# Transposes of the first half of the attention weights emitted before two quantisation slots and half of P·V, in an AdaLN transformer layer on eight cores

## The reference

```python
mod = (_silu(c) @ wmod).reshape(4, 6, 1, -1)          # sa, ca, ga, sb, cb, gb
h = _layernorm(x) * (1 + ca) + sa
k = h @ Wk.T ; q = h @ Wq.T ; v = h @ Wv.T
ak = k @ Wa.T
alpha = softmax(q @ ak.T)                             # 4096 x 4096 in each sequence
out = alpha @ (v @ Wb.T)
x = x + ga * out
h = _layernorm(x) * (1 + cb) + sb
# per-tensor: wq = clip(round(w / scale), -128, 127) * scale, scale = max|w| / 127
h = gelu(h @ quant(W_fc).T + b_fc + 2 * (h @ A_fc.T) @ B_fc.T)
x = x + gb * (h @ quant(W_proj).T + b_proj + 2 * (h @ A_proj.T) @ B_proj.T)
```

## Time and profile before

| | us |
|---|---|
| median of the timed runs (2) | 3236.74 |
| lowest, highest | 3222.4, 3251.07 |
| the profiled execution, device time | 3184.89 |
| its span on the slowest core (core 5) | 3183.3 |
| the spans of its eight cores | 3171.0 to 3183.3 |
| attention stage within that span, from the first eA to the last PV1 | 1233.4 to 2317.5 |

### The profile page before, as it was taken

How to read it: one execution, slowest core, us unless ns; L and a number is a source line. 1 busy time by engine, 2 the same in 40 slices (tenths; PEclk the granted TensorE clock), 3 DMA queues, 4 the chain that set the end, 5 groups by cost and what they waited for, 6 DMA issues and landing times.

```text
span 3183.3 us, 24979 instructions; the slowest of 8 cores (3171.0 to 3183.3 us)
## 1 busy us (share of the span) xinstructions
PE 1730.6 (54%) x7994; PEld 764.1 (24%) x7994; DVE 1001.1 (31%) x1773; ACT 763.1 (24%) x1325; POOL 432.7 (14%) x585
## 2 busy tenths in 40 slices
PE   3620040426666556455664465654526858858588
PEld 1210010112222222222222222222212323323233
DVE  3420333434444543444344434344311020110201
ACT  2310001032222231333233333233303122031220
POOL 0001222213333100111111112112200000000000
PEclk9855575757787768777777777777757979979799
DMA  4500424232222220121112212112151113112130
GB/s 142 169 13 5 139 86 136 71 116 69 68 70 68 70 63 30 53 73 70 60 57 77 72 60 73 57 58 78 60 167 54 59 51 95 60 50 63 47 99 27
DMA packets 92297, 233.40 MB, mean 73 GB/s; under 512 B 25380, under 2 KB 25509, under 8 KB 92152
## 3 DMA queue, kind: packets, MB, share of 16 engines
q1 hardware_dynamic: 65000, 160.33, 16.8%
q0 software_dynamic: 27168, 71.47, 6.4%
HBM read 193.85 MB, written 37.88 MB: 73 GB/s over the span
## 4 chain that ended last, share of the span: by engine, by line
PE 33%; DMA 23%; DVE 15%; issue 12%; ACT 10%; POOL 4%; SPq 1%; DVEq 1%; ACTq 0%; POOLq 0%
PE pO L1436 7%; DMA amst<-wpj_in 6%; PE pO L1198 5%; PE pE L1394 5%; PE pE L1101 5%; DMA wfcst<-wfcq_sc 4%; PE pE L1126 4%; ACT h_stage L729 3%; DVE qkf L960 2%; DMA wm<-wmod_in 2%; POOL qt L936 2%; DMA amst<-wfc_in 2%; PE pE L742 2%; ACT qkf L930 2%; DMA bfcT_sc<-lora 2%
## 5 line engine op out<-in xcount | busy, mean ns | idle before, releaser
L936 POOL TENSOR_TENSOR qt<-qt,qkf 128x1024 f32<-128x1024 f32 x64 | 149.9, 2342 | 939.5 <-ACT qkf L930 911.3
L1394 PE MATMUL pE<-h,wfcst 128*128 128x512 bf16 x1024 | 248.6, 386 | 51.8 <-DMA wfcst<-wfcq_sc 39.1
L1436 PE MATMUL pO<-wpj_sb,hid 128*128 128x512 bf16 x1024 | 226.4, 379 | 15.8 <-DVE outb L1452 12.0
L1101 PE MATMUL pE<-ak_fm,q_stg 128*128 128x512 bf16 x512 | 148.9, 462 | 142.2 <-DMA q_stg<-q_sc 110.0
L1198 PE MATMUL pO<-u_tm,alphaT 128*128 128x512 bf16 x512 | 152.2, 470 | 22.3 <-DVE alphaT L1077 22.3
L621 DVE TENSOR_REDUCE amx<-amst 128x1 f32<-128x256 f32 x256 | 106.7, 417 | 169.2 <-DMA amst<-wpj_in 111.8
L930 ACT ACTIVATE qkf<-qki 128x512 f32<-128x512 int32 x128 | 80.6, 629 | 309.3 <-DVE qki L927 309.3
L742 PE MATMUL pE<-h_stage,wkaT 128*128 128x512 bf16 x512 | 130.9, 423 | 30.3 <-ACT h_stage L729 30.3
L1409 ACT ACTIVATE hid<-pE,bfc_col 128x512 bf16<-128x512 f32 x128 | 88.0, 687 | 231.5 <-PE pE L1402 231.5
L1069 PE MATMUL pT<-idb,alphaA 128*128 128x128 bf16 x256 | 28.1, 278 | 207.0 <-DVE qbf L1011 201.0
L1394 PEld LDWEIGHTS pE<-h,wfcst 128*128 128x128 bf16 x1024 | 91.9, 98 | 183.0 <-issue 94.9
(11 more groups left out here) (187 smaller groups left out, 2660.3 us busy)
## 6 DMA issues: line engine op xcount, KB each, us to landing
wfcst<-wfcq_sc SPq DMA_DIRECT2D x128, 256.0 KB, 2.6
wm<-wmod_in SPq DMA_DIRECT2D x32, 768.0 KB, 4.7
x_st<-x_in SPq DMA_DIRECT2D x48, 512.0 KB, 4.2
amst<-wfc_in POOLq DMA_DIRECT2D x128, 128.0 KB, 2.5
amst<-wpj_in POOLq DMA_DIRECT2D x128, 128.0 KB, 2.5
wst<-wfc_in SPq DMA_DIRECT2D x32, 512.0 KB, 3.4
wst<-wpj_in SPq DMA_DIRECT2D x32, 512.0 KB, 4.0
wfcq_sc<-qbf POOLq DMA_DIRECT2D x32, 256.0 KB, 2.3
```

The lines of the kernel that those rows point to most:

```text
L936: t_dd = em("gpsimd", lambda e, qt=qt, qkf=qkf: e.tensor_tensor(out=qt[:], in0=qt[:], in1=qkf[:], op=OP.subtract), waits=[("s", t_kf)], in ...
L1101: t_eA = em("tensor", lambda e, oc=oc, jb=jb, p=p: e.matmul(out=s.pE[:, jb * 512:(jb + 1) * 512], lhsT=s.q_stage[p][:, oc * 128:(oc + 1) * ...
L1394: t_mm = em("tensor", lambda e, ic=ic, oc=oc, p=p, sl=sl: e.matmul(out=s.pE[:, sl * 512:(sl + 1) * 512], lhsT=wfcst[p][:, ic * 128:(ic + 1 ...
L1436: t_mm = em("tensor", lambda e, tt=tt, vc=vc, hc=hc: e.matmul(out=s.pO[:, vc * 512:(vc + 1) * 512], lhsT=hid[:, hc * 512 + tt * 128:hc * 5 ...
```

## The change

The block of transA moves up on TensorE and on VectorE: from the end of the loop's pass to right behind linv, ahead of P3, PV1 and P4. The bookkeeping moves with it: `st["alphaT_ev"]` is set only after PV1 of the tile before has been emitted, so PV1's waits are what they were. The `pump1()` of P4 stays behind PV1. No instruction is added or removed, and the lists of ScalarE, GpSimd and SyncE keep their order.

```diff
             st["linv"] = t_linv
+            tA, evA = emit_trans(0, ic, s.alphaA, t_rs, "v")
+            st["transA_done"] = tA
             pump1()
             if ic > 0:
                 self._emit_pv(ic - 1, st, emit_trans, part=1)
-            pump1()
-            tA, evA = emit_trans(0, ic, s.alphaA, t_rs, "v")
-            st["transA_done"] = tA
             st["alphaT_ev"] = evA
             st["_ic_linv"] = t_linv
+            pump1()
```

## The result

| | before | after |
|---|---|---|
| median of the timed runs | 3197.81 us (36) | 3226.69 us (37) |
| lowest, highest | 3184.21, 3260.06 | 3217.77, 3305.25 |
| profiled execution, span of its slowest core | 3183.3 us (core 5) | 3232.0 us (core 2) |

The ratio of after to before is 1.0098, 95% interval 1.0076 to 1.012: about 31 us slower. The forecast was +56 us. Two things went into that miss: the two runs known then had a median of 3236.7 for the kernel before, where 36 runs give 3197.8 (39 us), and the change cost less than the 56 forecast (29 us between the medians, 31 by the ratio, so 25 to 27 us). The first decided that the time left the range: with 3197.8 as its start the same range would have been 3219 to 3287.

What follows compares the result with a forecast made beforehand. The prediction took VectorE's chain of slots through the q load to eA as the bound. Fourteen passes at 3.7 us, plus 2.2 and 1.7, gave +56 us: 3237 to 3293 us, 1.7% slower, range 3258 to 3326.

Steps and rivals of the forecast that it cites:

- The chain that bounds the pass: In each attention pass: mB, exponential, rs, e1 of P3, P4 and P1, q load, eA, next mB; PV1 and transA lie beside it.
- The gain at transA's old place, 0: At the pass's end, removing transA's two groups and copies gains 0; the wait returns as longer idle before eA.
- +2.2 at P3: On VectorE, transA's two copies ahead of P3 start its e1 at 8.5 us after mB instead of 6.25.
- PV1's length: On TensorE, PV1, starting at 8.62 after an idle stretch, takes 9.3 us instead of 7.07 and ends at 17.9.
- The lower bound of 8.3: PV1's shortest length: 5.3 us at the low clock, counted from transA, leave PV1 2.5 of them.
- The rule I set aside: The Trainium skill's: TensorE's slow start is an amount of time under activity, so transposes use it up; total about 43 us.
- +3.7 at P4, of which 1.5 from s2 behind PV1: On VectorE, P4's e1 waits behind s2, held by PV1, and starts at 19.6 instead of 15.87, including the 2.2.
- From there the old distances hold: After P4's e1: 9.62 us to e1 of P1, 1.72 to the q load's issue, 3.97 to eA, unchanged.
- The first and the last pass: The first pass, without PV1, costs 2.2 us; the last, through transB's second group and PV0, costs 1.7.
- The first rival: Only VectorE's delay counts, or PV1 ends before 16.4: 2.2 us a pass, 35 in all (43 at PV1's bound); chance 0.22.
- The time put on the median: Whole kernel: the profiled execution lies 52 us under the timed median, so 56 us are added to 3237, giving 3293.
- The third rival: TensorE's 7.64 us idle before eA swallows the shift: not slower, 3216 to 3240 us; chance 0.05.

## Why the prediction was right and wrong, step by step

- *The chain that bounds the pass* was right, and is shown from three sides: a delay on VectorE alone costs the time of the change, PV1 5.8 late costs 0.5, and an early q load takes 8.4 off the pass.
- *The gain at transA's old place, 0*: right. The transposes' wait for L1011 fell by 194.3 us, and TensorE got it back ahead of transA (96.7) and of eA (125.0; in ic 1 to 14 it idles 7.4 to 8.6 there before and 16.0 to 17.4 after).
- *+2.2 at P3*: right, 8.46 against 6.30 in the mean. The start of PV1 at 8.62 was right to the hundredth.
- *PV1's length: the step of the cost that failed.* "I take 9.3, nearer to PV0". It is 7.79 in the mean, 7.15 to 7.44 in 8 of the 14 passes and 8.32 to 8.80 in the other 6. The lower bound of 8.3 fits the 6 and was too high for the 8. It rested on 5.3 us at the low clock from one eA, and that eA, 9.74, was nearly the longest: in the 14 passes of the trace of before eA takes 8.69 to 9.78, which is 3.2 to 5.4 at the low clock, and 3.2 would have put the bound at 7.3. The rule I set aside in favour of PV0's rows would have given the better number. What had spoken for PV0, its transposes 1.95 ahead, was perhaps a poor likeness, since an idle stretch of 0.94 lies between those and PV0; no run tests that.
- *+3.7 at P4, of which 1.5 from s2 behind PV1*: mis-sized because of it. It is +2.49 (18.43 against 15.94), so 0.3 from PV1 and not 1.5. In the 8 short passes PV1 ends by 16.1, and s2 decides nothing; in the 6 long ones P4 stands 0.7 to 1.2 later.
- *"From there the old distances hold"*: not quite. From P4's +2.49 to the pass's +2.02 about 0.45 come back, and eA (9.21 for 9.34) and PV0 (9.29 for 9.60) are shorter by that much in sum. A pure delay of VectorE shows the same give-back, 0.36 of 2.33, so it isn't a merit of the new order.
- *The first and the last pass*: 3.2 for 2.2, and 2.0 for 1.7.
- *The sum*: 14 x 2.02 + 5.2 = 33.5, where 14 x 3.7 + 3.9 = 56 was forecast. The first rival, "only VectorE's delay counts, or PV1 warms up early", at 35 us and with a chance of 0.22, comes nearest. That its 35 fits so well is in part luck: it leaves out both the 0.3 a pass that the late PV1s cost and the 0.45 that came back, and the two nearly cancel.
- *The time put on the median* also failed, and it alone decided that the time left the range: 3237 was the median of two runs, 1.2% above what 36 give. The profiled execution, 3185, lay near the lowest of them, 3184. The range had 14 us for that spread; it needed some 40.
- *The third rival*, a shift swallowed by the idle before eA, was rightly small: that idle ends with a load which is itself tied to the chain; eA came later by the shift (34.01 for 31.54).

## What to carry to other kernels

Before moving work into a gap, find out which engine's list carries the chain, and price the move by what it puts ahead of the next link there: here two copies of 0.69 with the transposes they wait for were 2.2 us, while a late start of 7 us of matmuls was almost free. A long wait in the list (302.6 us) says nothing of what its removal brings if the engine then stands before a later event; look for the event that ends the last idle stretch of the pass, here a load queued behind another load's wait. Take that away, then look for what holds the next step, and try the move again: the same edit was a loss of 2.0 us a pass, still a loss of 2.6 with the load out of the way, and a gain of 6.8 once the slots ahead of mA had moved too.

## What the runs showed of the hardware that was not expected

The time at 1.2 GHz after an idle stretch isn't one number, even with the same idle and the same instructions: PV1 took 7.15 to 8.80 in the changed kernel, in changing turns (7.40, 7.22, 8.39, 7.35, 8.80, 7.44, 7.15, 8.32, 7.30, 8.39 in successive passes), and a steady 8.58 to 8.78 in nearly all passes when it alone was late. Counted from the first instruction after the idle stretch, full clock was back after 2.8 to 3.5 us or after 5.3 to 6.2 (slowest cores of these two kernels), and the mean of 7.79 is the length of no pass. I take it that the length of a pass decides how its matmuls meet the clock, but no run shows it. A delay of 0.79, 2.33 or 4.03 us on the chain lengthened the pass by 0.49, 1.97 or 3.89, and PV1 behind the same transposes took 7.79 in the mean and cost 0.3 us at P4 in one arrangement, 8.49 and 0.8 in another.
